# Reordering the written-out step list of a decoder layer: keys and values of the second group earlier, two query parts later, some output projections one unit earlier

## The chip, the cores and the metric

The kernel runs on one core of a Trainium2 chip. The metric is device time in microseconds (us) of one launch; the lower the better. The core has five engines: TensorE (PE in the profile, with its weight loads as PEld), VectorE (DVE), ScalarE (ACT), GpSimd (POOL) and SyncE (SP), which only issues DMAs here.

## The reference, cut to what matters

The input x is 16 sequences of 128 tokens of 256 channels. Three blocks follow each other, each on the layer-normed x and added to x.

```python
x = x + attn(layernorm(x), ...)      # 16 heads, latent of 72 columns
x = x + xattn(layernorm(x), ctx)     # bidirectional RWKV sums over the context, times a sigmoid gate
x = x + ffn(layernorm(x), ...)       # 8 experts, 2 per token, gate/up/down
```

The attention, which the change touches:

```python
Wdkv = x @ latent_w + latent_b                                  # keys and values in one, 72 wide
q = einsum('btc,hcl->bhtl', x, Wd_w) + Wd_b
scores = einsum('bhtl,bsl->bhts', q, Wdkv) / 4                  # causal
y = einsum('bhts,bsl->bhtl', softmax(scores), Wdkv)
z = transpose(y).reshape(b, t, 16 * 72)
return z @ out_w + out_b
```

## The kernel before, in words

**Order of the work.** A string, STEPS (line 75), lists every step of the attention and cross-attention by name, and schedule() (line 163) turns it into the list ORDER. All five engine programs walk the same list (SP at 563, PE at 791, ACT at 994, DVE at 1336, POOL at 1539), and each runs its own share of each step, in that order, holding at semaphores for what other engines or DMAs must have done. So a step that is moved in the string moves in the queue of every engine that has a share of it, and an instruction that waits holds up everything behind it on its engine, and nothing on the others.

**Units of the attention.** A unit is one sequence and four heads; there are 64, numbered n. Up to unit 39 they come in blocks of eight that cover two sequences (units 0 to 7 are sequences 0 and 1, units 8 to 15 are 2 and 3, and so on; PAIRED in line 27). The steps of a unit: S.n, the masked scores (PE, 659), then the row maximum (DVE, 1118) and four exps (ACT, 896); N.n, the reciprocal of the sums (DVE, 1123) and the scaling of the probabilities (POOL, 1448); T.n, four transposes (PE, 676) and their copy into PT (ACT, 903); Y.n, the mix with the values (PE, 683), the copy of the result into ZT (DVE, 1127), and the packing (SP, 507): after every second unit of the paired blocks, four DMAs of 72 KB that move ZT, which lies by head, into zP, where the 16*72 rows of z fill 128 partitions. T.n runs two units behind S.n, and ACT's exps of unit n wait for T of unit n-3, since there are three EB buffers; the scores use two PSUM banks, so S.n also waits for the exps of n-2.

**Queries.** q.k.i computes part i of the queries of the sequences 2k and 2k+1 for all heads (PE, 645; five parts of two tiles, the last of one), ACT adds the bias and copies to qP (888), and SP moves each tile with a DMA of 128 KB into qT (500), where they lie by head. Each part waits on PE for ACT's copy of the part before it, because both use the bank QB (line 651). S.8k, the first unit of block k, waits for all nine tiles of block k (line 667).

**Keys and values.** kt.g makes the keys of the four sequences of group g (PE, 615: six matmuls of 512 columns; ACT's copy at 875), va.g transposes them into values (PE, 625), and vb.g copies those (DVE, 1105). Group 1 is first used by unit 16. They share the bank TR with the transposes of the normed x, tx (PE, 605; ACT, 864; DVE, 1098).

**Output projection.** O.b.i is part i of the projection of sequence b (PE, 706: three, two, two and two pairs of the nine row blocks of zP). Its part 0 waits until all four packings of the sequence's block have landed (lines 711 to 716); for sequence 0 the last of them follows Y.7, for sequence 2 it follows Y.15, for sequence 8 Y.39. add.i adds two projected sequences to x (DVE, 1138).

**Cross-attention.** w1 to w8, wa and wb are exps, scans, sums, reciprocals and transposes of the context; ctx.g loads 512 KB of it (SP, 486), behind a wait for w1 of the group before (DVE, 1150). SP's queue is in order too: ctx.2 and ctx.3 hold back the query tiles and packings that stand behind them.

**Behind the attention** (from about 360 us) come the experts, 23 tiles of 256 rows, on PE nearly without a gap.

Of the kernel before, what the change touches and what calls it, by code (L numbers as in the profile page):

```python
# [5 lines left out]
B, T, C = 16, 128, 256  # L6
# [72 lines left out]
S.1 va.0 rs.1.1.0.4 nmb.1.1.0.4 vb.0 w2.0.0 N.0 qd.2 xn.1.1.0.0 N.1 xn.1.1.0.2 w3.0.0 w6.0.0  # L79
S.2 qd.3 T.0 w4.0.0 w5.0.0 tx.1.1.0.4.0 w1.0.1 N.2 q.1.0  # L80
S.3 w7.0.0 q.1.1 Y.0 tx.1.1.0.4.1 T.1
S.4 q.1.2 w8.0.0.0 w2.0.1 q.1.3 Y.1 N.3 T.2 w3.0.1 w4.0.1
S.5 q.1.4 w5.0.1 N.4 Y.2 N.5 T.3
S.6 w8.0.0.1 w8.0.0.2 Y.3 w8.0.0.3 xb.2 xb.3 xb.0 T.4 w1.1.0
S.7 T.5 wa.0.0 Y.4
S.8 N.6 N.7 q.2.0 wb.0.0
S.9 T.6 bn.1.2.0.0 w6.0.1 Y.5 w7.0.1 w8.0.1.0 q.2.1 bn.1.2.0.2
S.10 kt.1 T.7 Y.6 q.2.2 N.8 w2.1.0 w3.1.0 Y.7 T.8 N.9 agg.1.2.0.4 rs.1.2.0.4
S.11 va.1 bn.1.3.0.0 ctx.2 vb.1 bn.1.3.0.2
S.12 Y.8 N.10 N.11 w4.1.0 w5.1.0 T.9 agg.1.3.0.4 xb.1 rs.1.3.0.4 w8.0.1.1 w8.0.1.2 w1.1.1 q.2.3 Y.9 N.12 T.10  # L90
S.13 w8.0.1.3 wa.0.1
S.14 O.0.0 T.11 Y.10 q.2.4 N.13 wb.0.1 w6.1.0
S.15 O.0.1 T.12 Y.11 w7.1.0 w8.1.0.0 N.14 N.15 Y.12 w2.1.1 O.0.2 T.13
S.16 nmb.1.2.0.4 w3.1.1 w4.1.1 q.3.0 w5.1.1 Y.13 O.0.3 T.14
S.17 w8.1.0.1 q.3.1 N.16 Y.14 O.1.0 O.1.1 w8.1.0.2 w8.1.0.3 w1.2.0 wa.1.0 T.15
S.18 N.17
S.19 T.16 q.3.2 N.18 Y.15 O.1.2 Y.16 xn.1.2.0.0 xn.1.2.0.2 wb.1.0 w6.1.1 w7.1.1 add.0 T.17 w8.1.1.0 O.1.3 tx.1.2.0.4.0 q.3.3 N.19 w2.2.0 T.18
S.20 Y.17
S.21 w3.2.0 w4.2.0 N.20 ctx.3 N.21 tx.1.2.0.4.1 T.19
S.22 w5.2.0 Y.18 w1.2.1 w8.1.1.1 O.2.0 kt.2 q.3.4 N.22 T.20 Y.19 w8.1.1.2 w8.1.1.3  # L100
S.23 va.2 vb.2 O.2.1 T.21 Y.20 wa.1.1
S.24 q.4.0 wb.1.1 Y.21 T.22 O.2.2 xb.4 w6.2.0 N.23
S.25 w7.2.0 w8.2.0.0
S.26 q.4.1 xb.5 N.24 Y.22 w2.2.1 T.23 O.2.3 w3.2.1 O.3.0 O.3.1 O.3.2 O.3.3 w4.2.1 w5.2.1 N.25 N.26 add.1 T.24
S.27 Y.23 bn.2.0.0.0 bn.2.0.0.2 agg.2.0.0.4 rs.2.0.0.4 q.4.2 N.27 Y.24 w1.3.0 T.25 q.4.3 nr.0.0.4 sig.0.0.0 w8.2.0.1
# [13 lines left out]
S.41 bn.2.1.0.0  # L119
S.42 T.39 q.6.1 Y.38  # L120
S.43 Y.39 O.7.1 T.40 w5.3.1 N.41 w8.3.0.3 wa.3.0 N.42 O.7.2 O.7.3 q.6.2 add.3 bn.2.1.0.2 agg.2.1.0.4 rs.2.1.0.4 va.3 Y.40 vb.3 N.43 T.41
S.44 nr.1.0.4 T.42 sig.1.0.0 x2.1.0.0.0 sig.1.0.2 x2.1.0.2.0 q.6.3 Y.41 out.1.0.4 wb.3.0 w6.3.1
S.45 N.44 T.43 O.8.0 O.8.1 bn.3.1.0.0 bn.3.1.0.2
S.46 N.45 Y.42 q.6.4 agg.3.1.0.4 O.8.2 O.8.3 rs.3.1.0.4 Y.43 T.44 nmb.3.1.0.4 xn.3.1.0.0 xn.3.1.0.2
S.47 w7.3.1 N.46 w8.3.1.0 O.9.0 O.9.1 O.9.2 Y.44
S.48 add.4 xd.1.0.4 O.9.3 N.47 T.45 tx.3.1.0.4.0 O.10.0 O.10.1 N.48 T.46 w8.3.1.1 w8.3.1.2 w8.3.1.3 q.7.0 Y.45 tx.3.1.0.4.1
# [1502 lines left out]
```

## Time and profile before

| what | value |
|---|---|
| median of three runs | 611.88 us |
| the three runs | 609.05, 611.88, 617.22 us |
| the profiled execution, its own time | 617.22 us |
| its span, first to last instruction | 615.6 us |
| mean granted TensorE clock | 0.957 of full |

The profiled execution is the slowest of the three runs. Times inside it count from the start of the span. What lies outside the span is 617.22 - 615.6 = 1.6 us. PE, PEld, DVE, ACT and POOL have busy times in the rows; SPq stands for SP's queue, whose entries are DMA issues.

### The profile page before, as it was taken

To read this page: it belongs to the slowest core of one execution; us is meant where nothing else is said; L and a number is where in the kernel's file an instruction comes from. 1 tells how busy PE (TensorE), PEld (TensorE's weight loads), DVE (VectorE), ACT (ScalarE), POOL (GpSimd) and SP (SyncE) were. 2 spreads that over 40 slices of the span, in tenths; PEclk is the share of its full clock that TensorE was granted. 3 is DMA by queue.
4 is the path that set the end of the run, shared out by engine and by line. 5 is a ranking of instruction groups with operands and counts; after the bars stand their busy time and mean duration, and the time that the engine had idled before them with its cause. 6 is when DMAs were issued, how large, how long until landed. Compare 5 with 4: busy or idle time off the path is not lost.

```text
span 615.6 us, 11029 instructions
## 1 busy us (share of the span) xinstructions
PE 543.3 (88%) x3728; PEld 478.9 (78%) x3728; DVE 401.9 (65%) x778; ACT 364.0 (59%) x993; POOL 338.4 (55%) x289
## 2 busy tenths in 40 slices
PE   0898989999999999999894966889989999999991
PEld 0786767867878878888582655889989999999991
DVE  3467696685888767655576344667847776786750
ACT  4376756765776666555652242546847776767650
POOL 3454876645581876616456540727274667666644
PEclk9999999999999999999998785789999999999997
DMA  7315343563355435443234473428598898898710
GB/s 203 145 32 97 64 73 83 69 100 54 66 132 72 64 55 71 117 64 63 42 93 110 128 228 122 120 53 246 154 306 201 229 229 223 224 221 219 173 31 2
DMA packets 54435, 76.63 MB, mean 124 GB/s; under 512 B 11305, under 2 KB 42794, under 8 KB 54122
## 3 DMA queue, kind: packets, MB, share of 16 engines
q1 hardware_dynamic: 43106, 63.91, 41.9%
q0 software_dynamic: 10384, 11.86, 10.2%
q8 instruction: 30, 0.49, 0.3%
q14 instruction: 27, 0.22, 0.2%
q10 hardware_dynamic: 888, 0.15, 0.1%
HBM read 50.21 MB, written 10.40 MB: 98 GB/s over the span
## 4 chain that ended last, share of the span: by engine, by line
PE 60%; issue 9%; DVE 9%; POOL 8%; DMA 5%; ACT 4%; SPq 3%; another core or an unknown queue 0%; POOLq 0%; DVEq 0%; ACTq 0%
PE P L594 25%; PE PO L594 9%; PE PO L718 7%; PE P L672 5%; PE P L690 5%; PE P L680 3%; SPq L518 2%; POOL EB L1451 2%; POOL cxa L1508 2%; DMA qT<-qP 2%; ACT EB L901 2%; POOL xs L1494 1%; DMA arena<-wd 1%; PE P L756 1%; DVE small L1121 1%
## 5 line engine op out<-in xcount | busy, mean ns | idle before, releaser
L594 PE MATMUL P<-GT,WF 128*128 128x256 f32 x1104 | 145.7, 291 | 7.1 <-DVE WF L1049 4.9
L594 PEld LDWEIGHTS P<-GT,WF 128*128 128x128 f32 x1104 | 139.9, 198 | 7.8 <-DVE WF L1049 5.3
L901 ACT ACTIVATE EB<-P,small 128x128 f32<-128x128 f32 x256 | 90.4, 367 | 77.8 <-DVE small L1121 58.0
L1451 POOL TENSOR_TENSOR EB<-EB,small 128x512 f32<-128x512 f32 x64 | 79.3, 1249 | 90.7 <-DVE small L1125 90.6
L1535 POOL DMA_INDIRECT out<-Y,TK x46 | 79.5, 1728 | 65.4 <-DMA out<-Y,TK 33.8
L690 PE MATMUL P<-PT,V 128*72 128x512 f32 x128 | 67.9, 612 | 11.8 <-ACT PT L906 10.6
L672 PEld LDWEIGHTS P<-KT,qT 72*128 72x128 f32 x512 | 66.8, 192 | 12.2 <-DMA qT<-qP 6.7
L594 PE MATMUL PO<-WF,HR 128*128 128x256 f32 x552 | 71.6, 288 | 4.0 <-issue 4.0
L594 PEld LDWEIGHTS PO<-WF,HR 128*128 128x128 f32 x552 | 69.2, 196 | 4.3 <-issue 4.3
L672 PE MATMUL P<-KT,qT 72*128 72x128 f32 x512 | 68.1, 276 | 4.7 <-DMA qT<-qP 3.8
L1136 DVE COPY ZT<-P 72x512 f32<-72x512 f32 x64 | 43.3, 677 | 43.8 <-PE P L690 38.3
L718 PE MATMUL PO<-Ow,zP 128*128 128x256 f32 x270 | 67.6, 391 | 2.0 <-DMA zP<-ZT 1.9
L1508 POOL DMA_INDIRECT cxa<-xd,TK x46 | 54.8, 1191 | 25.5 <-issue 13.1
L718 PEld LDWEIGHTS PO<-Ow,zP 128*128 128x128 f32 x270 | 50.5, 195 | 16.3 <-issue 10.7
L1121 DVE TENSOR_REDUCE small<-P 128x4 f32<-128x512 f32 x64 | 43.3, 677 | 23.7 <-PE P L672 23.0
L1049 DVE TENSOR_TENSOR WF<-arena,WF 128x1024 fp32r<-128x1024 f32 x36 | 43.8, 1223 | 18.3 <-ACT WF L966 17.4
L906 ACT ACTIVATE PT<-P 128x512 f32<-128x512 f32 x64 | 38.7, 605 | 28.2 <-PE P L680 28.2
L1494 POOL DMA_INDIRECT xs<-TKS,SL x32 | 33.2, 1037 | 35.9 <-DVE TKS L1256 25.6
L901 ACT ACTIVATION_READ_ACCUMULATOR EB<-P,small 128x1 f32 x256 | 52.6, 205 | 0.0
L1049 DVE TENSOR_TENSOR WF<-WR,WF 128x1024 fp32r<-128x1024 f32 x33 | 40.0, 1222 | 11.7 <-ACT WF L966 11.0
L680 PEld LDWEIGHTS P<-ident,EB 128*128 128x128 f32 x256 | 31.1, 143 | 20.6 <-issue 10.6
L680 PE MATMUL P<-ident,EB 128*128 128x128 f32 x256 | 39.4, 277 | 3.4 <-POOL EB L1451 3.2
(176 smaller groups left out, 921.4 us busy)
## 6 DMA issues: line engine op xcount, KB each, us to landing
arena<-wf SPq DMA_DIRECT2D x33, 512.0 KB
WR<-wf SPq DMA_DIRECT2D x33, 512.0 KB
qT<-qP SPq DMA_DIRECT2D x63, 128.0 KB
zP<-ZT SPq DMA_DIRECT2D x80, 72.0 KB
zP<-ZT SPq DMA_DIRECT2D x80, 36.0 KB
X<-x SPq DMA_DIRECT2D x4, 512.0 KB, 6.0
cxa<-ctxin SPq DMA_DIRECT2D x4, 512.0 KB, 5.8
out<-X SPq DMA_DIRECT2D x3, 512.0 KB, 5.3
```

The source lines that it names most:

```text
L594: r = e.matmul(o, lt(a), rt_(b), start=start and n == 0, stop=stop and n == 2, skip_group_check=skip)
L672: p = e.matmul(S[:, 128 * j:128 * j + 128], qT[k % 2][:, 4 * hq + j, c:c + 128], KT[g % 2][:, r:r + 128], start=False, stop=True, skip_gro ...
L680: p = e.transpose(PTB[:, 128 * j:128 * j + 128], EB[n % 3][:, j, :], ident[:, :])
L690: e.matmul(YB[0:L, :], V[g % 2][:, b % GB, :], PT[n % 2][:, :], start=True, stop=True).then_inc(s_Y, 1)
L718: p = e.matmul(o, zP[b // NB % 2][:, m, 128 * (b % NB):128 * (b % NB) + 128], Ow[:, m, :], start=m == 0, stop=m == NQ - 1)
L901: e.activation(EB[i][:, j, :], S[:, 128 * j:128 * j + 128], ACT.Exp, bias=NM[i][:, j:j + 1], accum_out=SM[i][:, j:j + 1]).then_inc(s_exp, 1)
L1049: return e.tensor_tensor(o, src, hi.bitcast(fp32), ALU.subtract)
L1121: e.tensor_reduce(NM[n % 3], SB[n % 2][:, :].rearrange("p (h s) -> p h s", h=4), AX.X, ALU.max, negate=True).then_inc(s_max, 1)
L1136: e.tensor_copy(ZT[buf][:, :, c:c + 128], YB[0:L, :].rearrange("p (h t) -> p h t", h=4)).then_inc(s_z, 1)
L1451: e.tensor_tensor(EB[i][:, :, :], EB[i][:, :, :], SM[i].unsqueeze(2).broadcast_to([128, 4, 128]), ALU.mult).then_inc(s_prob, 1)
L1508: e.indirect_dma_start(XG[i][:, a_, :], None, xd[0:(TN * 3 // 4, TN + 1)[phase(j)], :], bass.IndirectOffsetOnAxis(ap=TK[:, j, a_, 0:1].bit ...
L1535: e.indirect_dma_start(outr, bass.IndirectOffsetOnAxis(ap=TK[:, j, a_, 0:1].bitcast(i32), axis=0), Y[j % 2][:, a_, :], None, bounds_check= ...
```

## The change

Only the string of steps changes; no instruction is added or removed. In the diff S.n begins a line; the other names are the steps explained above (N, T, Y, q, O, kt, va, vb; w..., bn, agg, rs, nmb, xn, tx, sig, x2, out belong to the norms and the cross-attention). Lines in which nothing moved are left out.

```diff
-S.4 q.1.2 w8.0.0.0 w2.0.1 q.1.3 Y.1 N.3 T.2 w3.0.1 w4.0.1
-S.5 q.1.4 w5.0.1 N.4 Y.2 N.5 T.3
-S.6 w8.0.0.1 w8.0.0.2 Y.3 w8.0.0.3 xb.2 xb.3 xb.0 T.4 w1.1.0
+S.4 q.1.2 w8.0.0.0 w2.0.1 Y.1 N.3 T.2 w3.0.1 kt.1 w4.0.1
+S.5 w5.0.1 N.4 Y.2 va.1 N.5 q.1.3 T.3
+S.6 w8.0.0.1 w8.0.0.2 q.1.4 Y.3 w8.0.0.3 xb.2 xb.3 xb.0 T.4 w1.1.0
 S.7 T.5 wa.0.0 Y.4
 S.8 N.6 N.7 q.2.0 wb.0.0
-S.9 T.6 bn.1.2.0.0 w6.0.1 Y.5 w7.0.1 w8.0.1.0 q.2.1 bn.1.2.0.2
-S.10 kt.1 T.7 Y.6 q.2.2 N.8 w2.1.0 w3.1.0 Y.7 T.8 N.9 agg.1.2.0.4 rs.1.2.0.4
-S.11 va.1 bn.1.3.0.0 ctx.2 vb.1 bn.1.3.0.2
-S.12 Y.8 N.10 N.11 w4.1.0 w5.1.0 T.9 agg.1.3.0.4 xb.1 rs.1.3.0.4 w8.0.1.1 w8.0.1.2 w1.1.1 q.2.3 Y.9 N.12 T.10
+S.9 T.6 bn.1.2.0.0 w6.0.1 Y.5 vb.1 w7.0.1 w8.0.1.0 q.2.1 bn.1.2.0.2
+S.10 T.7 Y.6 q.2.2 N.8 w2.1.0 w3.1.0 Y.7 T.8 N.9 agg.1.2.0.4 rs.1.2.0.4
+S.11 bn.1.3.0.0 ctx.2 bn.1.3.0.2
+S.12 Y.8 N.10 N.11 w4.1.0 w5.1.0 T.9 agg.1.3.0.4 xb.1 rs.1.3.0.4 w8.0.1.1 w8.0.1.2 w1.1.1 q.2.3 Y.9 N.12 O.0.0 T.10
 S.13 w8.0.1.3 wa.0.1
-S.14 O.0.0 T.11 Y.10 q.2.4 N.13 wb.0.1 w6.1.0
-S.15 O.0.1 T.12 Y.11 w7.1.0 w8.1.0.0 N.14 N.15 Y.12 w2.1.1 O.0.2 T.13
+S.14 T.11 O.0.1 Y.10 q.2.4 N.13 wb.0.1 w6.1.0
+S.15 T.12 O.0.2 Y.11 w7.1.0 w8.1.0.0 N.14 N.15 Y.12 w2.1.1 T.13
...
-S.21 w3.2.0 w4.2.0 N.20 ctx.3 N.21 tx.1.2.0.4.1 T.19
-S.22 w5.2.0 Y.18 w1.2.1 w8.1.1.1 O.2.0 kt.2 q.3.4 N.22 T.20 Y.19 w8.1.1.2 w8.1.1.3
-S.23 va.2 vb.2 O.2.1 T.21 Y.20 wa.1.1
-S.24 q.4.0 wb.1.1 Y.21 T.22 O.2.2 xb.4 w6.2.0 N.23
+S.21 w3.2.0 w4.2.0 N.20 O.2.0 ctx.3 N.21 tx.1.2.0.4.1 T.19
+S.22 w5.2.0 Y.18 w1.2.1 w8.1.1.1 O.2.1 kt.2 q.3.4 N.22 T.20 Y.19 w8.1.1.2 w8.1.1.3
+S.23 va.2 vb.2 T.21 O.2.2 Y.20 wa.1.1
+S.24 q.4.0 wb.1.1 Y.21 T.22 xb.4 w6.2.0 N.23
...
-S.44 nr.1.0.4 T.42 sig.1.0.0 x2.1.0.0.0 sig.1.0.2 x2.1.0.2.0 q.6.3 Y.41 out.1.0.4 wb.3.0 w6.3.1
-S.45 N.44 T.43 O.8.0 O.8.1 bn.3.1.0.0 bn.3.1.0.2
+S.44 nr.1.0.4 T.42 sig.1.0.0 O.8.0 x2.1.0.0.0 sig.1.0.2 x2.1.0.2.0 q.6.3 Y.41 out.1.0.4 wb.3.0 w6.3.1
+S.45 O.8.1 N.44 T.43 bn.3.1.0.0 bn.3.1.0.2
```

## Rows read from the trace of the kernel before

**Rows 1.** Page, busy time of TensorE over the span, share, instructions.

```profile
PE 543.3 (88%) x3728; PEld 478.9 (78%) x3728; DVE 401.9 (65%) x778; ACT 364.0 (59%) x993; POOL 338.4 (55%) x289
```

**Rows 2.** Chain that ended last, 50 to 100 us: start us, us, what.

```profile
50.76 1.70 PE P L594 x12
...
53.36 0.69 DVE ZT L1136
...
58.89 4.85 DMA qT<-qP
...
71.73 1.38 PE P L594 x6
...
75.29 3.01 POOL EB L1451
...
81.52 0.11 DVE V L1109
...
98.50 1.08 PE P L690 x2
```

**Rows 3.** Windows: length, PE, PEld, DVE, ACT, POOL busy, clock, DMA share, GB/s.

```profile
44.00:63.00 19.00, 16.23 (x109) 12.70 (x107) 13.61 (x20) 12.89 (x47) 10.20 (x9) 1.00 0.55 106
69.00:88.00 19.00, 15.85 (x102) 11.83 (x101) 15.73 (x36) 12.72 (x47) 12.67 (x10) 1.00 0.54 74
87.00:89.00 2.00, 1.99 (x16) 1.91 (x17) 2.00 (x3) 1.11 (x3) 2.00 (x2) 1.00 0.20 28
119.00:128.00 9.00, 9.00 (x66) 7.70 (x64) 7.26 (x11) 7.21 (x26) 3.85 (x3) 1.00 0.56 74
229.00:238.00 9.00, 9.00 (x61) 7.70 (x60) 7.44 (x20) 3.87 (x15) 5.38 (x5) 1.00 0.52 73
```

**Rows 4.** Timeline of SP's queue: start us, us, DMA issues.

```profile
78.26 2.86 SPq L518 DMA_DIRECT2D zP<-ZT  x4
...
117.57 1.27 SPq L505 DMA_DIRECT2D qT<-qP  x2
118.88 2.87 SPq L518 DMA_DIRECT2D zP<-ZT  x4
...
133.22 0.60 SPq L489 DMA_DIRECT2D cxa<-ctxin  x1
...
228.39 1.30 SPq L505 DMA_DIRECT2D qT<-qP  x2
230.43 2.86 SPq L518 DMA_DIRECT2D zP<-ZT  x4
```

**Rows 5.** Timeline of PE: start us, us, line, operation, idle before and releaser.

```profile
89.75 1.46 PE L718 MATMUL PO<-Ow,zP 128*128 128x256 f32 x6
...
125.36 0.60 PE L612 MATMUL P<-ident,XN 128*128 128x128 f32 x4
...
128.46 1.53 PE L718 MATMUL PO<-Ow,zP 128*128 128x256 f32 x6
...
139.78 1.16 PE L672 MATMUL P<-KT,qT 72*128 72x128 f32 x8 [2.46 <-DMA qT<-qP]
...
236.99 1.66 PE L594 MATMUL P<-xnTb,Wd 128*128 128x256 f32 x12
...
241.35 2.32 PE L718 MATMUL PO<-Ow,zP 128*128 128x256 f32 x10
...
335.50 1.98 PE L690 MATMUL P<-PT,V 128*72 128x512 f32 x2 [6.24 <-ACT PT L906]
```

**Rows 6.** Timeline of PE's weight loads, at sequence 2's projection.

```profile
128.43 1.16 PEld L718 LDWEIGHTS PO<-Ow,zP 128*128 128x128 f32 x6 [0.92 <-issue]
```

**Rows 7.** Timeline of DVE, the row maximum of unit 22.

```profile
129.53 0.68 DVE L1121 TENSOR_REDUCE small<-P 128x4 f32<-128x512 f32 x1
```

**Rows 8.** Chain that ended last, at 312 us.

```profile
311.97 2.14 DMA zP<-ZT
```

**Rows 9.** Window of PE alone: length, busy, clock, DMA share, GB/s.

```profile
344.00:347.00 3.00, 3.00 (x7) 0.50 0.87 290
```

## The prediction

> **What bounds the kernel.** Read the busy times first: PE is busy for 543.3 of 615.6 us [rows 1], so it is the engine to ask about, but the change moves work around and adds none, so the share alone says nothing. What counts is where PE waits, and whether a step that is moved forward on it finds its inputs there. For that I read the chain that ended last, in order of time, and beside it the timelines of PE and of SP's queue, and then the DMA share in windows, since two of PE's waits (the first unit of a block, and part 0 of a projection) are for DMAs that SP issues.
>
> The reader is to see three things. In the opening stretch the chain leaves PE: the third query part of block 1 runs at 50.76, DVE can copy Y.1 only at 53.36, and unit 8 waits for the last query tile, issued at 58.89 and landed 4.85 us later [rows 2]. From there to the experts the chain is mostly PE, in pieces of 0.4 to 2 us, with short excursions to POOL and DVE such as the 3.01 us at 75.29 [rows 2]; what PE loses there, the end loses. And the DMAs of this stage have a queue of their own: in each of the stretches 44 to 63, 69 to 88, 119 to 128 and 229 to 238 us the share stands at 0.52 to 0.56 with 73 to 106 GB/s [rows 3], a plateau that holds for as long as query tiles and packings are outstanding. On it a packing lands when the bytes ahead of it have gone, not some fixed time after its issue.
>
> **How late a packing lands.** Behind 69 us SP issues six query tiles of 128 KB and eight packing DMAs of 72 KB, some 1.38 MB, and at 74 GB/s this takes the 19 us of the window; the last four are issued from 78.26 [rows 4] and are the last to land: in 87 to 89 the mean share is down to 0.20 [rows 3], so they land near 88.0. Sequence 2's last packing is issued from 118.88, behind two query tiles at 117.57 [rows 4]. That is 0.56 MB, 7.6 us at 74 GB/s, from about 119: data through at 126.6. The projection that needs it starts at 128.46 [rows 5], and its weight loads had stood idle for 0.92 us [rows 6]. No engine is named as releaser and its other conditions were met long before, so I read 128.4 as the landing, 10.8 us behind the first tile's issue. Sequence 8's last packing has the same two tiles ahead of it, issued at 228.39 [rows 4], so it lands at about 239.2.
>
> **Part 1, the opening (q.1.3 and q.1.4 later, kt.1 and va.1 earlier).** PE no longer waits for ACT's copy before Y.1: it runs Y.1 at about 49.0, DVE copies it when its scan ends at 50.4 instead of 53.36, and units 5 to 7 come about 1.7 us earlier, kt.1's 1.38 us of matmuls [rows 2] included, which fit into what was PE's wait. But unit 8 needs the nine query tiles. By hand, engine after engine, ACT ends the copy of q.1.4 at 59.6, 0.7 us later than the issue at 58.89 [rows 2], and the bytes ahead of it are the same, so on the plateau its landing stays at 63.7. Gain 0. Bounds: 0, and +0.7 if the tile again takes 4.85 us from its issue.
>
> **Part 2, keys and values gone from units 10 and 11.** Here kt.1 cost PE its 1.38 us at 71.73, on the chain; and the copy of the values stands on DVE's piece of the chain with 0.11 us and the gap behind it, 0.3 us [rows 2]. PE's four short transposes go with it. What is late next is DVE's copy of Y.6 and POOL's N.8, which both follow PE, so the chain keeps its shape and moves by -1.7 us at unit 12. kt.1's new neighbours pay nothing, since that stretch ends in the wait of part 1. The DMAs of this stretch do not move: they start with q.2.0, at most 0.5 us earlier.
>
> **Part 3, O.0.0 ahead of T.10.** With part 2 PE is through Y.9 at 84.9. The packing behind Y.7 lands at about 87.7 (88.0 less what q.2.0 gained, 0.3). So PE stands for 2.8 us, and behind it in its queue stand T.10 and units 13 and 14; before, O.0.0 came after both, at 89.75 [rows 5], when the data was there. It then takes 1.3 us (1.46 less the overlap), and the scores of unit 13 end at 90.7, where DVE took them before at 90.3: the 1.7 us of part 2 are gone and 0.4 beyond. Later something comes back: O.0.2 no longer lies between Y.12 (98.50 [rows 2]) and unit 16; four matmuls of that kind take 0.86. Net at unit 16: +0.4 - 0.9 = -0.5. Bounds for parts 2 and 3 together: -2.2 if the packing has landed when PE comes, +0.7 if unit 16 then waits for its query tiles.
>
> **Part 4, O.2.0 in unit 21's line.** PE comes to it where the transposes of 125.36 ran [rows 5], and the packing lands at 128.4: 2.9 us of standing, 1.2 us of matmuls. Behind it stand the transposes, T.19 and unit 22 (0.44, 0.44 and 1.13 us), so unit 22's scores end at 131.7, and its row maximum starts there instead of at 129.53 [rows 7]: 2.1 us later. That matters beyond PE. Behind this maximum DVE has the scan that w1.2.1 waits for, behind w1.2.1 stands SP's load ctx.3 at 133.22 [rows 4], behind that the last query tile of block 3, and on it PE's wait of 2.46 us before unit 24 at 139.78 [rows 5]. All of it moves by 2.1. Behind unit 24 PE then has O.2.2 no more, 0.86 us. Net +1.2. Bounds: -0.9 (packing early, O.2.2 done inside the old wait) and +2.1.
>
> **Part 5, O.8.0 ahead of q.6.3.** PE comes to it at 237.1, just where q.6.3 ran (236.99), and not at 241.35 [rows 5]. The packing lands at 239.2: 2.1 us at most. Its last bytes are thinner (share 0.52 against 0.56, rows 3), so I take off half a microsecond: +1.6, all on PE's unbroken piece of the chain. Bounds: 0 and +2.5. What q.6.3 feeds, ACT's copy, had slack of some 3 us.
>
> **Sum.** 0 - 0.5 + 1.2 + 1.6 = +2.3 us. Made against the profiled execution: 617.22 becomes 619.5. It is the slowest of three; carried to the median, 611.88 + 2.3 = 614.2 us.
>
> **Rival A, the packings land early.** If a packing that is issued lands as the one at 311.97 did, 2.14 us after its last issue [rows 8], then those of Y.7, Y.15 and Y.39 are there at 83.3, 123.9 and 235.5, before PE comes each time. Then no projection waits: 0 - 2.2 - 0.9 + 0 = -3.1, 608.8 us. For it: nothing in the trace before had to wait long at these places. Against: 0.92 us of idle at 128.43 [rows 6], and the plateau [rows 3]; at 311.97 the queue was short. This is how the Trainium skill would have it: the page SBUF — State Buffer (The DMA setup-cost knee) gives a DMA about 2 us and its bytes over 436 GB/s, an estimate of 2.2 us for a packing. The plateau here is 74 GB/s, so the trace does not agree for this kind of transfer.
>
> **Rival B, the clock falls in the new waits: slower.** Behind an idle time of 6.24 us PE ran its two matmuls in 1.98 us, about twice their full-speed time [rows 5], and in 344 to 347 the clock still stood at 0.50 [rows 9], so that from 332 to 347 it ran at 1.2 instead of 2.4 GHz. The new waits, 2.8 us at unit 12 and 2.9 us at unit 21, lie where PE sets the pace; 15 us at half clock cost 7.5 us of it. One fall: 614.2 + 7.5 = 621.7 us; both: 629.2. Against: behind the wait of 2.46 us the eight matmuls took 1.16 us [rows 5], full speed. It decides when a new wait comes to about 3 us or more and joins another. The Trainium skill has a rule on this side, in TensorE: Matmul & The Clock Gate (HAM oscillation — how this bites in real kernels): waits for a DMA between bursts of matmuls throttle the engine again. By that rule this change is the wrong way round, since it puts waits inside a dense stretch.
>
> **How the numbers follow.** Forecast (waits at the projections, gains elsewhere, sum near +2.3, own range 611 to 618): 0.64. Rival A, 608.8: 0.24. Rival B: 0.12, most of it one fall. The bounds add to -3.1 and, with 0.7 + 0.7 + 2.1 + 2.5, to +6.0: 608.8 to 617.9. Medians of a kernel whose runs lie from 609.05 to 617.22 scatter by a microsecond or two themselves, so the range is 608.0 to 619.5. About 2% (12.2 us) is what a measurement of this kernel can tell from no change. Slower by more needs over 624.1, both clock falls or worse: 0.05. Faster by more needs under 599.6, which no case here gives: 0.02. Within 2%: 0.93.
>
> **What would show it.** Right: unit 8 starts at 63.5 to 64.5 behind a wait for qT of over 1.5 us; line 718's first group starts at 87 to 88.5 with an idle time of 2 to 3 us ahead of it, sequence 2's again at about 128, less 0.5, behind some 3 us of idle, and sequence 8's behind 1 to 2 us; the load ctx.3 is issued some 1.6 us later than at 133.22 and unit 24 follows it. Wrong: projections with no idle ahead of them (rival A), a clock under 1.00 between 60 and 290 us (rival B), a landing of the packings that moves with their issue, or a gain at unit 8, which would mean that the tiles were not limited by bytes.

## The result, and the profile after

| | median us | runs |
|---|---|---|
| before, in the same comparison | 614.27 | 6 (609.05 to 617.36) |
| after | 623.31 | 6 (618.26 to 627.97) |

The ratio of after to before is 1.0142, with a 95% interval of 1.0091 to 1.0193: slower by 1.4%. The interval leaves out 1, but the change is under the 2% from which this measurement calls one certain. The forecast was 614.2 us in a range of 608.0 to 619.5. It had the direction, and about a quarter of the size. The profiled execution of after took 621.63 us, span 620.0; before's was 617.22 and 615.6. The record lists 21 more executions of after beside the six: twenty from 618.91 to 631.17 us, and one of 1093.32 us whose cause is not known. Over all comparisons of this study the kernel before ran 73 times, with a median of 615.33 us and the middle half of the runs between 613.2 and 617.9. So the 611.88 on which the forecast was put, a median of three, was itself low by 3.5 us.

The ratios leave out runs more than 1.5% above the fastest of the same kernel; the medians are over all runs.

The first view is the page of after: TensorE's busy time (first row) and its group of line 718, the output projections.

```profile
PE 543.4 (88%) x3728; PEld 479.6 (77%) x3728; DVE 401.7 (65%) x778; ACT 364.9 (59%) x993; POOL 343.5 (55%) x289
...
L718 PE MATMUL PO<-Ow,zP 128*128 128x256 f32 x270 | 70.3, 401 | 9.7 <-DMA zP<-ZT 9.7
```

Busy PE is what it was, 543.4 against 543.3 us [rows 1]. The work is the same; what is new stands in the last column: 9.7 us of idle time ahead of projections, all released by packings. In the page of before the same group had 67.6 us busy and 2.0 idle. The timeline of PE shows where (start us, us, line, operation, count, idle before and its releaser):

```profile
49.11 1.64 PE L594 MATMUL P<-xnTb,Lw 128*72 128x512 f32 x6
...
63.26 1.16 PE L672 MATMUL P<-KT,qT 72*128 72x128 f32 x8 [2.26 <-DMA qT<-qP]
64.18 2.66 PE L594 MATMUL P<-xnTb,Wd 128*128 128x256 f32 x12
...
85.14 1.08 PE L690 MATMUL P<-PT,V 128*72 128x512 f32 x2 [1.52 <-ACT PT L906]
88.61 2.90 PE L718 MATMUL PO<-Ow,zP 128*128 128x256 f32 x6 [2.39 <-DMA zP<-ZT]
...
131.57 1.76 PE L718 MATMUL PO<-Ow,zP 128*128 128x256 f32 x6 [3.57 <-DMA zP<-ZT]
133.12 1.06 PE L612 MATMUL P<-ident,XN 128*128 128x128 f32 x4
133.97 1.06 PE L680 MATMUL P<-ident,EB 128*128 128x128 f32 x4
...
146.54 1.16 PE L672 MATMUL P<-KT,qT 72*128 72x128 f32 x8 [0.92 <-DMA qT<-qP]
...
246.14 1.53 PE L718 MATMUL PO<-Ow,zP 128*128 128x256 f32 x6 [1.82 <-DMA zP<-ZT]
...
306.73 4.08 PE L718 MATMUL PO<-Ow,zP 128*128 128x256 f32 x10 [0.29 <-DMA zP<-ZT]
```

Read each row twice. The bracket at its end is the wait that was forecast: 2.39, 3.57 and 1.82 us at the three projections, against 2.8, 2.9 and up to 2.1. The duration is what was not: the six matmuls that took 1.46 us [rows 5] take 2.90 at 88.61; the four transposes of line 612 take 1.06, not 0.60 [rows 5]; ten matmuls of line 718, 2.32 at 241.35 [rows 5], take 4.08. The windows of after say why (length, busy times with counts, granted clock, DMA share, GB/s):

```profile
61.00:64.00 3.00, 0.74 (x6) 0.74 (x7) 0.75 (x2) 1.99 (x9) 0.69 (x1) 1.00 0.48 113
64.00:67.00 3.00, 3.00 (x18) 3.00 (x18) 0.84 (x3) 1.63 (x9) 1.69 (x2) 0.58 0.01 3
...
86.00:87.00 1.00, 0.22 (x1) 0.00 (x0) 1.00 (x2) 0.83 (x3) 1.00 (x2) 1.00 0.54 83
87.00:88.00 1.00, 0.00 (x0) 0.00 (x0) 1.00 (x3) 0.00 (x0) 1.00 (x2) 1.00 0.05 6
88.00:89.00 1.00, 0.39 (x1) 0.42 (x2) 1.00 (x2) 0.00 (x0) 1.00 (x2) 0.68 0.00 0
88.00:91.00 3.00, 2.39 (x6) 1.98 (x7) 1.72 (x3) 0.00 (x0) 2.93 (x3) 0.56 0.17 58
...
133.00:136.00 3.00, 3.00 (x14) 2.78 (x13) 0.69 (x1) 1.19 (x2) 0.18 (x1) 0.50 0.56 70
```

Two things stand there. Behind the waits at 63, 88 and 131 us the granted clock falls from 1.00 to its other level, 0.50, for some three microseconds (0.58, 0.56 and 0.50 as means of three). And from 87 to 88 us the DMA engines are nearly still, share 0.05, while PE waits on until 88.61. The chain of after, in order of time, has the same stretch from the other side:

```profile
79.23 0.67 SPq L518
79.90 0.04 issue
79.94 8.53 DMA zP<-ZT
88.47 0.14 issue
88.61 2.90 PE PO L718 x6
```

The packing is released at 88.47. Its last bytes are not gone at 87, although the mean share is near nothing: one row of packets, each behind the other, is still under way, as finer windows of after show.

```profile
87.20:87.50 0.30, 0.00 (x0) 0.00 (x0) 0.30 (x1) 0.00 (x0) 0.30 (x2) 1.00 0.10 14
87.50:88.00 0.50, 0.00 (x0) 0.00 (x0) 0.50 (x2) 0.00 (x0) 0.50 (x1) 1.00 0.01 0
```

By the packet records of the trace the last packet of 1 KB ends at 87.65, and PE starts 0.96 us later.

### The profile page after: what moved, and what is told of

The parts are those of the page before. It is cut to its first block, busy times and chain, and to the rows that moved or that the text cites. A ratio compares the mean times of both kernels' runs of the same rounds, so it can differ in the third digit from the quotient of the medians.

```text
span 620.0 us, 11028 instructions
## 1 busy us (share of the span) xinstructions
PE 543.4 (88%) x3728; PEld 479.6 (77%) x3728; DVE 401.7 (65%) x778; ACT 364.9 (59%) x993; POOL 343.5 (55%) x289
## 4 chain that ended last, share of the span: by engine, by line
PE 54%; POOL 12%; issue 11%; DMA 8%; DVE 7%; SPq 3%; ACT 2%; another core or an unknown queue 1%; POOLq 0%; DVEq 0%
PE P L594 22%; PE PO L594 7%; PE PO L718 7%; PE P L672 5%; PE P L690 5%; DMA zP<-ZT 3%; POOL EB L1451 3%; SPq L518 3%; POOL xs L1494 3%; PE P L680 3%; POOL cxa L1508 2%; DMA out<-Y,TK 1%; DMA arena<-wd 1%; PE P L665 1%; POOL out L1535 1%
## 5 line engine op out<-in xcount | busy, mean ns | idle before, releaser
L1451 POOL TENSOR_TENSOR EB<-EB,small 128x512 f32<-128x512 f32 x64 | 83.1, 1309 | 94.1 <-DVE small L1125 94.0
L1535 POOL DMA_INDIRECT out<-Y,TK x46 | 83.1, 1805 | 57.5 <-DMA out<-Y,TK 37.2
L718 PE MATMUL PO<-Ow,zP 128*128 128x256 f32 x270 | 70.3, 401 | 9.7 <-DMA zP<-ZT 9.7
L690 PE MATMUL P<-PT,V 128*72 128x512 f32 x128 | 66.8, 604 | 11.7 <-ACT PT L906 9.5
L594 PE MATMUL PO<-WF,HR 128*128 128x256 f32 x552 | 70.1, 284 | 4.1 <-issue 4.1
L594 PEld LDWEIGHTS PO<-WF,HR 128*128 128x128 f32 x552 | 67.8, 192 | 4.4 <-issue 4.4
L1508 POOL DMA_INDIRECT cxa<-xd,TK x46 | 51.0, 1108 | 25.9 <-DMA TK<-xs 13.1
L1494 POOL DMA_INDIRECT xs<-TKS,SL x32 | 34.7, 1084 | 35.9 <-DVE TKS L1256 25.6
L680 PEld LDWEIGHTS P<-ident,EB 128*128 128x128 f32 x256 | 31.8, 145 | 20.9 <-issue 11.6
L1049 DVE TENSOR_TENSOR WF<-WR,WF 128x1024 fp32r<-128x1024 f32 x33 | 40.0, 1222 | 11.7 <-ACT WF L966 11.3
```

Of the source, the lines that this page charges most:

```text
L594: r = e.matmul(o, lt(a), rt_(b), start=start and n == 0, stop=stop and n == 2, skip_group_check=skip)
L680: p = e.transpose(PTB[:, 128 * j:128 * j + 128], EB[n % 3][:, j, :], ident[:, :])
L690: e.matmul(YB[0:L, :], V[g % 2][:, b % GB, :], PT[n % 2][:, :], start=True, stop=True).then_inc(s_Y, 1)
L718: p = e.matmul(o, zP[b // NB % 2][:, m, 128 * (b % NB):128 * (b % NB) + 128], Ow[:, m, :], start=m == 0, stop=m == NQ - 1)
L1049: return e.tensor_tensor(o, src, hi.bitcast(fp32), ALU.subtract)
L1451: e.tensor_tensor(EB[i][:, :, :], EB[i][:, :, :], SM[i].unsqueeze(2).broadcast_to([128, 4, 128]), ALU.mult).then_inc(s_prob, 1)
```

## The experiments

The two profiled executions begin about a microsecond apart, so the traces are compared by when the scores of a unit start on PE, counted from those of unit 4, minus the same for the kernel before (us; minus is earlier). The last row is the rest of the span behind unit 63, for before 288.7. Columns: after; after again; filled; opening only; projections only; keys and values (two executions); sequence 0, 2 and 8 only; rows cut; columns cut.

| unit | after | again | filled | open. | proj. | k,v | k,v again | seq 0 | seq 2 | seq 8 | rows | columns |
|---|---|---|---|---|---|---|---|---|---|---|---|---|
| 5 | -1.9 | -1.9 | -1.9 | -1.9 | 0.0 | 1.4 | 1.4 | 0.0 | 0.0 | 0.0 | -1.9 | -1.9 |
| 8 | 0.6 | 0.4 | 1.7 | 4.5 | -0.3 | 0.3 | 0.3 | 1.6 | -0.3 | 1.1 | 0.8 | 0.7 |
| 9 | 2.1 | 0.4 | 1.7 | 6.6 | -0.2 | 0.4 | 0.4 | 1.6 | -0.2 | 1.0 | 0.8 | 0.7 |
| 12 | 0.5 | -1.2 | 0.0 | 4.9 | -0.2 | -1.1 | -1.1 | 1.6 | -0.2 | 1.0 | -0.9 | -1.0 |
| 13 | 5.6 | 5.4 | 4.8 | 4.8 | 5.5 | -1.2 | -1.2 | 6.9 | -0.2 | 1.0 | 6.1 | 4.5 |
| 16 | 3.6 | 3.9 | 2.8 | 4.8 | 4.2 | -1.0 | -1.1 | 5.7 | 1.2 | 1.3 | 4.3 | 3.3 |
| 21 | 3.6 | 4.0 | 2.8 | 4.8 | 4.2 | -0.9 | -1.0 | 5.7 | 1.2 | 1.4 | 4.2 | 3.3 |
| 22 | 9.9 | 11.4 | 7.7 | 4.8 | 11.4 | -0.9 | -1.0 | 5.7 | 7.8 | 1.4 | 9.2 | 6.0 |
| 24 | 7.8 | 9.6 | 5.2 | 5.0 | 9.8 | -0.1 | -1.1 | 6.2 | 6.3 | 1.9 | 7.0 | 3.7 |
| 25 | 7.0 | 8.8 | 4.4 | 8.0 | 9.0 | 2.7 | 2.1 | 7.8 | 5.5 | 3.5 | 6.1 | 2.8 |
| 27 | 8.2 | 9.9 | 5.5 | 8.0 | 10.2 | 2.7 | 2.1 | 7.8 | 6.7 | 3.5 | 7.3 | 4.0 |
| 46 | 10.2 | 11.9 | 8.1 | 8.1 | 12.1 | 2.7 | 2.1 | 7.9 | 6.7 | 5.4 | 9.3 | 6.0 |
| 63 | 11.7 | 13.3 | 9.6 | 10.2 | 13.6 | 4.7 | 4.3 | 10.0 | 6.7 | 6.7 | 11.2 | 7.8 |
| rest | 282.5 | 283.7 | 283.5 | 283.4 | 282.0 | 284.8 | 285.0 | 284.1 | 285.8 | 284.4 | 284.0 | 285.8 |

The last row is a warning: the rest is 3 to 7 us longer in the one trace of before than in all twelve others, though nothing in it was changed. The spans, 620.0 and 615.6, therefore hide most of what the attention lost against this trace (11.7 us), and only steps within the table are compared, not spans. The attention of that trace was a lucky one in turn: its clock records have no fall between 22.8 and 333.4 us. Every other kernel that leaves O.2.0 in its old place (opening only, keys and values twice, sequence 0, sequence 8) has one at unit 24, behind waits of 2.38 to 3.21 us, and all twelve but sequence 2 only lose 1.3 to 2.2 us behind unit 46, where no step differs. So the absolute numbers of the lower rows are too large for a typical execution; the steps from 12 to 16, 21 to 22 and 44 to 46 are what the change is read from.

**Opening only**, the change without its projections (here against after, two of the lines):

```diff
-S.12 Y.8 ... Y.9 N.12 O.0.0 T.10
+S.12 Y.8 ... Y.9 N.12 T.10
...
-S.44 nr.1.0.4 T.42 sig.1.0.0 O.8.0 x2.1.0.0.0 ...
+S.44 nr.1.0.4 T.42 sig.1.0.0 x2.1.0.0.0 ...
```

> The kernel after with all O steps back where they stood before; only q.1.3, q.1.4, kt.1, va.1 and vb.1 are moved. Unit starts are compared with before, both counted from unit 4. Theory (waits and a half-speed clock behind them): unit 8 at +0.6, unit 9 at +2.1 with the clock at 0.5 behind the wait, unit 12 at +0.5, unit 13 at about +0.5 and the end of the attention (unit 63) within 1 us of before; time within 1.5 us of before. Rival (the whole loss sits in the opening, the projections only show it): unit 13 at +4 or more and unit 63 near +10.

Measured: 615.7 us (10 runs) against 615.33 (25 runs), ratio 0.9992 [0.9946, 1.0038]. In its profiled execution, the longest of the ten at 621.57, the last query tile came late:

```profile
67.67 2.07 PE L672 MATMUL P<-KT,qT 72*128 72x128 f32 x8 [6.19 <-DMA qT<-qP]
```

A wait of 6.19 us, where after had 2.26 and after again 2.14 with the same steps ahead of it, and behind it scores at half clock (2.07 us, not 1.16). So the landing of unit 8's tiles varies between executions of the same steps by 4 us, more than the change moved it. Taken alone, this trace has the rival's numbers (unit 13 at +4.8, unit 63 at +10.2, where the theory wanted +0.5 and under 1). Two things speak against the rival all the same: the steps from unit 12 to 13, 21 to 22 and 44 to 46, where after loses 5.1, 6.3 and 2.1 us, are -0.1, 0.0 and 0.0 here, and the median of ten runs did not rise. What holds for every trace with the opening: the gain of units 5 to 7 is gone at unit 8, and the opening alone changes the median by nothing that can be told.

**Projections only**, the kernel before with the `O` steps of the change (two of the lines).

```diff
-S.14 O.0.0 T.11 Y.10 q.2.4 N.13 wb.0.1 w6.1.0
-S.15 O.0.1 T.12 Y.11 ... w2.1.1 O.0.2 T.13
+S.14 T.11 O.0.1 Y.10 q.2.4 N.13 wb.0.1 w6.1.0
+S.15 T.12 O.0.2 Y.11 ... w2.1.1 T.13
```

> The kernel before with only the O steps of sequences 0, 2 and 8 moved. Theory: no wait of 3 us before unit 8, full clock there; PE stands about 2 us before O.0.0, near 3.6 us before O.2.0 and 2 us before O.8.0, unit 16 at about +1 to +2, the step from unit 21 to unit 25 about +3.4, from 44 to 46 about +2.1, unit 63 at +6 to +8; time about 7 us over before. Rival (the loss sits in the opening): unit 63 within 1 us of before.

Measured: 618.55 us (10 runs), ratio 1.0051 [1.0009, 1.0094]. The three steps in the table: +5.7 from unit 12 to 13 with 1.3 given back by 16; +7.2 from 21 to 22, 2.4 back by 25, +1.2 at 27; +2.0 at 46. This is the loss of after, made without the opening. The ten runs spread from 613.75 to 625.85 and the profiled one was the second longest, 624.59, so the trace shows more than the median, which is 3.2 us up where about 7 was expected.

**Keys and values only**, `kt.1`, `va.1` and `vb.1` moved, twice (the lines that they leave).

```diff
-S.10 kt.1 T.7 Y.6 ...
-S.11 va.1 bn.1.3.0.0 ctx.2 vb.1 bn.1.3.0.2
+S.10 T.7 Y.6 ...
+S.11 bn.1.3.0.0 ctx.2 bn.1.3.0.2
```

> The kernel before with only kt.1, va.1 and vb.1 moved to units 4, 5 and 9; q.1.3 and q.1.4 stay. Theory: the matmuls fit into PE's wait for ACT, unit 8 stays at 0.0 to +0.3 with full clock behind it, unit 12 at -1.5 to -1.7, and the projection of sequence 0 then has to wait a little for its packing, so unit 16 at -0.5 to -1.5 and unit 63 the same; time 1 us under before. Rival (keys in the opening push the rest there): unit 8 at +1 or more and nothing gained at unit 12.

> The kernel before with kt.1, va.1 and vb.1 alone moved, once more. Theory (part 2 is right: what is taken from units 10 and 11 is a gain of PE): units 12 to 23 1.0 us early (range 0.7 to 1.5), and what follows is set by when query tiles land and the clock behind them, which changes from run to run; median 0 to 2.5 us under the kernel before, ratio 0.996 to 1.0. Rival (the load of the work on POOL and ACT takes the gain back in the median): ratio 1.000 to 1.004.

Measured: 613.87 us (10 runs), ratio 0.9966 [0.9923, 1.001], then 614.86 (12 runs), ratio 0.9992 [0.9952, 1.0031]. Both traces gain 1.5 us between unit 9 and unit 12 and keep 0.8 to 1.1 of it against before until unit 23. Then both lose 3 us at one place, behind a wait that before had too, 2.46 us [rows 5]:

```profile
139.72 2.07 PE L672 MATMUL P<-KT,qT 72*128 72x128 f32 x8 [3.21 <-DMA qT<-qP]
```

Eight scores in 2.07 us against before's 1.16 [rows 5]: half clock. The second execution shows it as well, behind a wait of 2.38 us, shorter than before's; and sequence 8 only, whose steps are those of before up to unit 44, loses 1.5 us there too. Both kernels' medians are below before's, by 1.5 and 0.3 us, but neither interval leaves out one.

**Filled**, after with matmuls on constants ahead of four waits, into banks that the next matmuls overwrite; they add work to PE and take none away.

```diff
                     pe.wait_ge(s_add, b // 2)
+                    for _ in range({0: 6, 2: 7, 8: 4}.get(b, 0)):
+                        e.matmul(o, Ow[:, 0, 0:128], Ow[:, 1, :], start=True, stop=True, skip_group_check=True)
                     z = packed_upto(b)
...
+                if n == 8:
+                    for _ in range(11):
+                        e.matmul(S[:, :], identr[:, :], maskr..., start=True, stop=False, skip_group_check=True)
                 if k:
                     pe.wait_ge(s_qd[k % 2], q_loaded(k))
```

> The kernel after, with matmuls that change no result put into PE's queue ahead of four waits: 11 repeats of the mask matmul before unit 8's wait, and 6, 7 and 4 extra matmuls into the quarter that is about to be overwritten, before the waits of O.0.0, O.2.0 and O.8.0. They fit into the waits. Theory (half-speed clock behind the waits costs some 4 to 5 us): the landings stay, the clock stays at 1.00 from 60 to 290 us, unit 9 at +0.6 instead of +2.1, unit 16 near +1 instead of +3.6, the step from 21 to 25 about +2 instead of +3.4. Rival (the clock plays no part, only the waits do): unit starts as in the kernel after, or later by what the extra matmuls stick out.

Measured: 621.81 us in one execution. The waits are still there, only filled, and the work behind them runs at full speed (timeline of PE; lines are shifted by 3 to 5):

```profile
65.66 1.16 PE L675 MATMUL P<-KT,qT 72*128 72x128 f32 x8 [0.84 <-DMA qT<-qP]
66.58 1.66 PE L594 MATMUL P<-xnTb,Wd 128*128 128x256 f32 x12
...
90.67 1.53 PE L723 MATMUL PO<-Ow,zP 128*128 128x256 f32 x6 [1.05 <-DMA zP<-ZT]
...
131.92 1.53 PE L723 MATMUL PO<-Ow,zP 128*128 128x256 f32 x6 [0.39 <-DMA zP<-ZT]
133.29 0.60 PE L612 MATMUL P<-ident,XN 128*128 128x128 f32 x4
```

The clock stood at 1.00 from 61 to 70, 84 to 94 and 130 to 139 us. Unit 9 loses nothing against unit 8 (after: 1.6), and from unit 21 to 25 the loss is 1.6 us instead of 3.4. From the start of O.0.0 to that of unit 13's scores are 2.04 us, in after 3.61. So the clock's share is 1.6 to 1.8 us at each of the three places. The rest of the loss is the wait itself, which fillers can't remove. Not all came as expected: unit 9 is at +1.7 and not at +0.6, unit 16 at +2.8 and not near +1, because unit 8's tiles and the packing of Y.7 landed about a microsecond later here, and against after the step from unit 12 to 16 is only 0.3 us shorter.

The same stretches give the price of a longer fall. From the start of O.2.0 to that of unit 25's scores are 17.7 and 17.8 us in the two traces without a fall there (filled, columns cut), 19.4 and 19.6 in the two where it lasts 3.4 us (after, rows cut), and 20.8 to 21.1 in the three where it lasts 6.8 us (after again, projections only, sequence 2).

**After again**, the changed kernel once more.

> The kernel after once more, unchanged, to see what repeats. Theory (waits for the packings, plus a half-speed clock behind waits of some 3 us): PE again stands before O.0.0, O.2.0 and O.8.0, units 13, 22 and 45 jump by about 5, 6 to 7 and 3.3 us against before, each time with the clock at 0.5 behind the first two; unit 63 at +9 to +14. Rival (the trace of after was one unlucky execution): one of the three jumps is missing, or the time is within 3 us of before.

Measured: 627.71 us (4 runs) against 616.13 (7 runs), ratio 1.0243 [1.0165, 1.0322]. Over both comparisons after has a median of 625.4 in ten runs, 10 us over the 615.33 of before. The trace has the same three waits (3.54, 3.55 and 1.78 us) but no fall of the clock behind unit 8, after a wait of 2.14 us there where after had 2.26: whether a wait of two to three microseconds lowers the clock is not decided by its length alone.

**One sequence at a time**: sequence 0, 2 or 8 only, each the kernel before with the `O` steps of one sequence moved.

> The kernel before with the parts of O.0 alone moved; everything else stands as it was. With all projections moved and the opening as before, unit 13's scores came 5.7 us later against unit 12's, and 4.2 us later by unit 16. Theory (each new wait at a projection is paid where it stands, one independent of the other): the same here, unit 13 5 to 6 us late, unit 16 4.2 late (range 3 to 5), and units 21, 24 and 44 as late as unit 16, within 1 us. Rival (waits that follow for other engines swallow the delay): under 1.5 us late at unit 44. Median: 2 to 4 us above the kernel before, ratio 1.003 to 1.007.

> The kernel before with the parts of O.2 alone moved. With all projections moved the step from unit 21 to unit 22 was 7.2 us longer and the one to unit 25 gave 2.4 back. Theory (each wait is paid where it stands): nothing up to unit 21, then 5 to 7 us late at unit 22 (3 to 5 if the clock stays at full speed behind the wait), 3 to 5 late at unit 25 and the same at unit 44. Rival (the wait at O.2.0 was so long only because the work ahead of it was late and so the data too): under 3 us late at unit 22 and under 1 at unit 25. Median: 2 to 5 us above the kernel before.

> The kernel before with the parts of O.8 alone moved. Theory: nothing up to unit 44, then 3.3 us late at unit 45 and 2.0 late at unit 46 (range 1.2 to 2.6), behind an idle time of 1.5 to 2.1 us ahead of O.8.0 for the packing. Rival (the packing had been late only because the queue was late in the runs with other edits): no idle time over 0.5 us there and less than 0.5 us late at unit 46. Median: within 3 us of the kernel before, too small for these rounds to tell from none.

Measured, with before at 615.19 us (35 runs): 619.29 (10 runs), ratio 0.9998 [0.9949, 1.0047]; 619.53 (10 runs), ratio 1.0066 [1.0021, 1.011]; 618.43 (10 runs), ratio 1.0062 [1.0021, 1.0104]. From the timelines of PE of sequence 0, 2 and 8 only, in this order:

```profile
89.47 2.90 PE L718 MATMUL PO<-Ow,zP 128*128 128x256 f32 x6 [2.20 <-DMA zP<-ZT]
```

```profile
129.49 2.90 PE L718 MATMUL PO<-Ow,zP 128*128 128x256 f32 x6 [2.70 <-DMA zP<-ZT]
```

```profile
242.57 1.53 PE L718 MATMUL PO<-Ow,zP 128*128 128x256 f32 x6 [1.75 <-DMA zP<-ZT]
```

Own steps in the table (in sequence 0 only another 2.2 us come behind unit 16, 1.6 of them with the fall at unit 24 that the other kernels have too): sequence 0 +4.1 from unit 12 to 16; sequence 2 +5.4 from unit 21 to 27; sequence 8 +2.0 from unit 44 to 46. In projections only they were 4.4, 6.0 and 2.0. Each wait is paid where it stands, whatever was late before. The rivals fall: the delay of sequence 0 is still there at unit 44, and sequence 2's wait is 2.70 us with PE only 1.2 us late. With sequence 0 the median rose by 4 us and the ratio did not, so for that part alone the time is not settled by the runs, only by the trace. Nor do the medians add up: the three parts raise them by 4.1, 4.3 and 3.2 us one by one, and by 3.2 together (projections only).

**Tiles cut**, after with fewer bytes ahead of the packing of sequence 2: the second tile of q.3.2 sends an eighth of its rows (112 KB less), or both of its tiles send half of every row (128 KB less, as many rows). What is not sent is left out of the result. The edit shown is the second.

```diff
-                    e.dma_start(qT[k % 2][8 * m:8 * m + 8, :, :], qP[:, m, :]).then_inc(s_qd[k % 2], 16)
+                    w = 128 if (k, i) == (3, 2) else 128 * NB
+                    e.dma_start(qT[k % 2][8 * m:8 * m + 8, :, 0:w], qP[:, m, 0:w]).then_inc(s_qd[k % 2], 16)
```

> The kernel after, with the second of the two query tiles ahead of sequence 2's last packing (q.3.2) sending one eighth of its rows: 112 of 128 rows of 1 KB are left out, so the queries of block 3 are incomplete. Theory (a packing lands when the rows ahead of it have gone): it lands 1.4 to 1.8 us earlier, and the wait before O.2.0 falls from about 3.6 to about 2 us. Rival (a packing needs a fixed time from its issue): the wait stays at 3.3 to 3.8 us.

> The kernel after, with both query tiles of q.3.2 sending only the first 128 of 256 columns: 256 rows as before, of 512 bytes, so the queries of sequence 7 are incomplete. If the bytes are the limit, as the prediction had it, 128 KB fewer bring the packing 1.4 to 1.8 us earlier, and the wait before O.2.0 to about 2 us. If the number of rows is the limit, nothing moves: a wait of 3.3 to 3.8 us.

Measured: 623.41 and 621.8 us in one execution each. PE's projection of sequence 2 in the two timelines, rows cut and then columns cut:

```profile
131.28 2.64 PE L721 MATMUL PO<-Ow,zP 128*128 128x256 f32 x6 [1.74 <-DMA zP<-ZT]
```

```profile
129.66 1.53 PE L719 MATMUL PO<-Ow,zP 128*128 128x256 f32 x6 [1.18 <-DMA zP<-ZT]
```

The wait of 3.57 (3.55) us fell by 1.8 and by 2.4. At the plateau's 74 GB/s [rows 3] 112 and 128 KB are 1.55 and 1.8 us. A measure that does not depend on when PE came is the time from the packing's first issue to PE's start: it is 9.3 to 10.2 us in the six executions with whole tiles in which PE waited, 8.3 with rows cut and 7.8 with columns cut. Fewer bytes ahead bring the packing forward by about their own time, and halving bytes with the row count kept does no less, so it is bytes, not rows, that hold the queue. With columns cut the clock did not fall at this place and the step from unit 21 to 22 was 2.7 us instead of 6.3. With rows cut it fell even behind 1.74 us, hence the 2.64 us of the matmuls.

**Packing on ACT**, after with the packings of Y.7, Y.15 and Y.39 issued by ScalarE instead of SyncE.

```diff
+                elif name == "Y" and a[0] in (7, 15, 39):
+                    pack_early(a[0])
...
-                if b < B - 1 and (nb == 1 or b % NB == NB - 1):
+                if b < B - 1 and (nb == 1 or b % NB == NB - 1) and n not in (7, 15, 39):
```

> The kernel after, with the packings behind Y.7, Y.15 and Y.39 issued from ACT's queue instead of SP's, so that they do not stand behind the query tiles. Theory (the landing is late because of what is ahead in SP's queue): they land 2 us or more earlier, the waits before O.0.0, O.2.0 and O.8.0 shrink to under 1.5 us, the clock stays at 1.00 there, and unit 63 comes 4 us or more earlier than in the kernel after, less what ACT's four issues (some 0.7 us each) delay the exps. Rival (packings are slow by themselves, whatever the queue): the waits stay within 0.5 us.

Measured: 625.53 us in one execution, with this timeline of PE:

```profile
88.56 2.88 PE L718 MATMUL PO<-Ow,zP 128*128 128x256 f32 x6 [1.60 <-DMA zP<-ZT]
...
131.88 1.46 PE L718 MATMUL PO<-Ow,zP 128*128 128x256 f32 x6
...
247.42 1.53 PE L718 MATMUL PO<-Ow,zP 128*128 128x256 f32 x6 [0.98 <-DMA zP<-ZT]
```

The waits shrink to 1.60, none and 0.98 us, and nothing is won: the projections start at 88.56, 131.88 and 247.42, not before those of after (88.61, 131.57, 246.14), since PE now comes later. Unit 21 is at +7.5 (after: 3.6) and unit 63 at +14.8, where 4 us less than in after was expected, and the clock falls behind the 1.60 us, where 1.00 was expected. At O.0.0 the packing itself lands no earlier either: it is issued at 77.90 and PE starts at 88.56, against 77.76 and 88.61. So another engine's queue does not carry it past the bytes in flight; at O.8.0, from 239.81 to 247.42, it saves 1.0 us of 8.6. ScalarE pays for it: its four issues take 2.85 us, and the normed x that stands behind them comes late, as the timelines of ACT and PE show.

```profile
119.81 2.85 ACTq L910 DMA_DIRECT2D zP<-ZT  x4
122.70 2.07 ACT L862 ACTIVATE XN<-X,small 128x256 f32<-128x256 f32 x4 [2.62 <-DVE ZT L1147]
```

```profile
124.83 0.66 PE L612 MATMUL P<-ident,XN 128*128 128x128 f32 x4 [2.12 <-ACT XN L862]
```

SyncE shows the same from its side: six query tiles take 16.42 us from 113.18; in after the same six take 13.55 us, from 113.11 to 126.66, with the packing's four issues among them.

```profile
113.18 16.42 SPq L505 DMA_DIRECT2D qT<-qP  x6
```

## Why the forecast was short, step by step

The step that failed is in parts 3 and 4: they charge a new wait for its length and price the matmuls, transposes and scores behind it at full clock, and the fall of the clock stands beside the sum as rival B with 0.12. The runs show a fall behind the new waits at O.0.0 and O.2.0, for 1.6 us at least at each. The second failure is part 3's landing of the packing of Y.7, read 2.0 us too early. The sign that the prediction itself named, a clock under 1.00 between 60 and 290 us, came.

**Part 1 was right in after and after again, in part by luck.** Units 5 to 7 came 1.9 us early (forecast 1.7), kt.1 ran in PE's old gap (49.11), and unit 8 was at +0.6, inside the bounds of 0 to +0.7, behind a wait of 2.26 us. What failed here was the cover of the waits: at half clock q.2.0 took 2.66 us instead of 1.66, and unit 9 was 1.6 us later still. After again shows the step without it. The bound of +0.7 is no bound: the same steps gave +4.5 in opening only, and before's own steps gave +1.6 and +1.1 in sequence 0 and 8 only.

**Part 2 was right.** -1.6 us from unit 9 to 12 in after, -1.7 in after again, -1.5 with keys and values only; forecast -1.7.

**Part 3: the landing was read too early, and the matmuls priced at full clock.** Forecast from unit 12's line to unit 16: -0.5 less -1.7, a loss of 1.2. Measured: 3.1 (after), 5.2 (after again), 4.4 and 4.1 without the opening. The landing "at about 87.7" took the end of the bytes, 88.0, for the landing. In before's own trace the last packet ends at 88.24, and in four traces PE started 0.9 to 1.1 us after the last packet's end (after 87.65 and 88.61; sequence 0 only 88.36 and 89.47; projections only 88.59 and 89.61; after again 87.94 and 88.86). For sequence 2 the prediction had such a gap before it, bytes through at 126.6 and landing at 128.4, and did not carry it over. In the frame of before, with after's earlier start of 1.1 us added, this projection started at 89.7, not 87.7, and PE came to it at 87.3, not 84.9, since unit 8 and the clock behind it had taken part 2's gain. The two errors are alike, so the wait of 2.39 us near the forecast 2.8 is in part luck; after again, where the gain held, PE waited 3.54. "It then takes 1.3 us" was the second: it took 2.90, and the clock stayed down behind it. The give-back by unit 16, forecast 0.9, was 1.3 without the opening, 2.0 in after and 1.4 in after again.

**Part 4: right wait, wrong price behind it.** Forecast 2.9 us of standing; 2.70 alone, 3.57 in after, where the tiles and packing of SP's queue were late with everything else:

```profile
121.36 2.87 SPq L518 DMA_DIRECT2D zP<-ZT  x4
...
140.29 0.60 SPq L489 DMA_DIRECT2D cxa<-ctxin  x1
```

From the packing's first issue to PE's start are 10.2 us here and 9.6 in before (118.88 [rows 4] to 128.46 [rows 5]). What stood in the sum as 1.2 us of matmuls and 2.0 of transposes and scores ran at half clock: from 131.57 to unit 22's row maximum are 5.2 us, as DVE's timeline shows, against 3.3 forecast.

```profile
136.78 0.69 DVE L1121 TENSOR_REDUCE small<-P 128x4 f32<-128x512 f32 x1 [1.25 <-PE P L672]
```

The chain over the scan and ctx.3 kept its order, but not its size: ctx.3 was issued at 140.29, 8.2 us later than 133.22 in the frame of before, where 2.1 had been forecast. Unit 24's wait shrank from 2.46 to 0.92, but from unit 16 to 25 the loss was 3.4 us instead of 1.2. Not in the sum at all was the 1.2 us at unit 27, which came with every kernel that moves O.2: PE waits there 0.95 us for POOL's scaling of the probabilities.

**Part 5 was right**: O.8.0 waited 1.82 us, started at 239.1 in before's frame, less the 8.2 us by which unit 44 was late (forecast 239.2), and the loss was 2.1 (forecast 1.6).

**The rivals.** Rival A, packings that land 2.14 us after their issue, is out: in after they took 6 to 8.5 us from it, and less when bytes ahead were taken away. Rival B had the right mechanism at the wrong size. It looked at the one fall in before ahead of 350 us, read as 15 us long (by the clock records 13.7), took 7.5 us as its only price and gave it 0.12. The falls behind the new waits are 3.4 or 6.8 us long and cost from 1.6 us to a little over 3. In after, after again, projections only and the single sequences every new wait at O.0.0 and O.2.0 had one: six matmuls in 2.90 us, or, at O.2.0 in after, in 1.76 with the transposes behind them at half speed. Its condition, a wait of about 3 us or more that joins another, was wrong too: 1.60 us (packing on ACT) and 1.74 (rows cut) were enough. The length alone does not decide it, since at unit 8 the clock fell behind 2.26 and 2.29 us and not behind 2.14, 2.35 and 2.47, and O.8.0's waits of 1.73 to 1.82 us had no fall in six traces. The Trainium skill's rule, in TensorE: Matmul & The Clock Gate (HAM oscillation — how this bites in real kernels), that waits for a DMA between bursts of matmuls throttle the engine again, agrees with these traces. A short fall per wait belonged in the forecast as a term, not beside it as an unlikely case.

**The sum**, for after at unit 63: 11.7 us against 2.3. The gap of 9.4 is 2.2 in parts 1 and 2 (the clock behind unit 8, 1.6, and its landing, 0.6), 1.9 in part 3, 2.2 in part 4, 1.2 at unit 27, 0.5 in part 5, and 1.4 behind unit 46, where ten matmuls at 306.73 took 4.08 us. That last term is not the change's: opening only and keys and values only lose 2 us there with before's steps. The median rose by 9.0 us in the first comparison and by 11.6 in the second. **The base** was the other error: 2.3 us on the median of 73 runs gives 617.6. That is 3.5 of the 9.1 us between the forecast and the measured median. The 5.6 us left are less than the 9.4 of the terms above, since these are counted against one trace whose attention was lucky; how much of each term a typical execution pays is not shown.

What stays open: why the median of projections only is up by just 3.2 us when its trace loses 12, and whether the shorter rest behind unit 63 belongs to the change or to one unlucky trace of before. The second is likelier, since opening only and both executions with keys and values have it too, but before was profiled once. A likely part of the first answer is the fall at unit 24: kernels that move O.2.0 wait there only 0.9 to 1.3 us and have none (packing on ACT apart), so they win back what a typical execution of before loses.

## What to carry to other kernels

Before a consumer is moved forward past the work that used to hide a transfer, work out the transfer's release, not the end of its bytes. Charge a new wait on the engine that sets the pace for its length, and price as a term of the sum that the work behind it runs at half clock. Moving producers into a gap that exists gained 1.5 us here in the traces, too little for the medians to show; moving consumers ahead of their data cost 2 to 6 us at each of three places in the traces, and issuing the transfers from another in-order queue bought none of it back in the one execution that tried it. Where runs of the same kernel lie 15 us apart, one trace and a median of three are a weak base; compare steps between the same two points of several traces.

## What the runs showed of the hardware that was not expected

- A packing's wait ended 0.9 to 1.1 us after its last packet in four traces (after: 87.65, PE at 88.61). The mean DMA share is near nothing half a microsecond before that packet ends (0.10 from 87.2 to 87.5).
- Waits of 1.60 to 6.19 us were followed by 3.4 or 6.8 us at the 1.2 GHz level, for 1.6 us to a little over 3. Length alone does not decide: at unit 8 the clock fell behind 2.26 and 2.29 us and not behind 2.14, 2.35 and 2.47; at unit 24 it fell behind 2.38 and not behind before's 2.46.
- Query tiles behind the same steps landed 2.1, 2.3 and 6.2 us after PE was ready for them in three executions.
- Issued from ScalarE's queue instead of SyncE's, the packing of Y.7 landed when it did before, 10.7 us behind its first issue (10.9 from SyncE). Its packets ran only from 82.77 to 87.59, although the first issue was at 77.90.
